# Local attention of the layers on packed columns: query blocks of 64 by 192 keys, cross blocks transposed in pairs, and values with exchanged halves

## The reference

```
def look_around(t):                     # the window before a window's own
    p = jnp.pad(t, ((0, 0), (0, 0), (1, 0), (0, 0), (0, 0)))
    return jnp.concatenate([p[:, :, :w], p[:, :, 1:]], axis=3)
sim = jnp.einsum('bhwid,bhwjd->bhwij', bq, bk)       # 128 queries, 256 keys
mask = (i < j) | (i > j + WINDOW) | (j == -1)
attn = jax.nn.softmax(jnp.where(mask, -jnp.finfo(sim.dtype).max, sim), axis=-1)
out = jnp.einsum('bhwij,bhwjd->bhwid', attn, bv)
...
h = shift_token(x); qkv = h @ wqkv; q, k = rotary_xpos(l2norm(q) * qs, l2norm(k) * ksc)
x = x + local_attention(q, k, v) @ wo
h = layernorm(shift_token(x)); a, g = jnp.split(h @ w1 + b1, 2, axis=-1)
x = x + (a * gelu(g)) @ w2 + b2
```

## Time and profile before

| | us |
|---|---|
| runs of the kernel | 2047.69 median of 3 (2045.26 to 2047.88) |
| the profiled execution | 2045.3, of it the span 2043.5 |
| busy: PE | 1900.0 (93%) |
| ACT | 1386.6 (68%) |
| DVE | 1327.4 (65%) |
| POOL | 960.7 (47%) |

### The profile page before, as it was taken

One profiled execution on the slowest core, in us unless ns is written; L12 is line 12 of the kernel. 1 busy time (PEld: TensorE's weight loads), 2 busy tenths in 40 slices (PEclk: granted clock), 3 DMA queues, 4 the chain that ended last, 5 costly groups with the idle time before them and its releaser, 6 DMA issues.

```text
span 2043.5 us, 42506 instructions
## 1 busy us (share of the span) xinstructions
PE 1900.0 (93%) x15184; PEld 1576.0 (77%) x15184; DVE 1327.4 (65%) x4125; ACT 1386.6 (68%) x3869; POOL 960.7 (47%) x1311
## 2 busy tenths in 40 slices
PE   6999999999999789999999999999999999999998
PEld 4778777777777668778788787787887878878777
DVE  4544543444443467777768777787777776877775
ACT  5886877778678465775766757657567575675764
POOL 2432442434243463644726537457265473663732
PEclk9999999999999889999999999999999999999999
DMA  3322231313225411010110101304101011010010
GB/s 127 109 80 66 75 118 44 97 60 88 92 66 162 151 39 32 19 43 12 45 45 12 42 22 37 104 6 161 55 6 52 22 45 55 22 42 27 31 33 27
DMA packets 122261, 121.10 MB, mean 59 GB/s; under 512 B 27188, under 2 KB 100804, under 8 KB 122052
## 3 DMA queue, kind: packets, MB, share of 16 engines
q1 hardware_dynamic: 118884, 112.10, 17.2%
q10 hardware_dynamic: 3168, 6.29, 0.9%
HBM read 72.72 MB, written 37.25 MB: 54 GB/s over the span
## 4 chain that ended last, share of the span: by engine, by line
PE 32%; DVE 20%; ACT 9%; issue 3%; POOL 3%; DVEq 0%; ACTq 0%; SPq 0%; POOLq 0%
PE f_bank L1383 11%; PE f_scores L1523 5%; PE f_scores L1461 4%; ACT f_prob L1598 4%; DVE f_u L1751 4%; PE f_bank L1509 4%; PE f_bank L1469 4%; DVE f_gu L1748 2%; PE f_o_bank L1484 2%; ACT f_u L1618 2%; PE f_bank L1434 2%; DVE y_tok L1734 2%; DVE y_tok L1740 1%; POOL f_prob L1336 1%; DVE f_rstd L1727 1%
## 5 line engine op out<-in xcount | busy, mean ns | idle before, releaser
L1336 POOL TENSOR_SCALAR f_prob<-f_prob,f_row_inv 128x256 f32<-128x256 f32 x512 | 263.0, 532 | 331.2 <-DVE f_row_inv L1694 331.1
L587 POOL TENSOR_SCALAR a_prob<-a_prob,a_row_inv,a_gate 128x128 f32<-128x128 f32 x512 | 224.4, 455 | 407.8 <-DVE a_row_inv L927 407.8
L1383 PE MATMUL f_bank<-weights,f_actT 128*128 128x512 f32 x1152 | 301.8, 406 | 1.6 <-DVE f_actT L1637 1.6
L1509 PE MATMUL f_bank<-f_hT,f_w 128*128 128x256 f32 x2112 | 276.2, 286 | 7.6 <-DVE f_gu L1748 7.6
L1509 PEld LDWEIGHTS f_bank<-f_hT,f_w 128*128 128x128 f32 x2112 | 261.9, 190 | 14.2 <-DVE f_gu L1748 10.7
L1598 ACT ACTIVATE f_prob<-f_scores,f_neg_max 128x256 f32<-128x256 f32 x512 | 235.8, 487 | 32.6 <-DVE f_neg_max L1686 31.6
L1383 PEld LDWEIGHTS f_bank<-weights,f_actT 128*128 128x128 f32 x1152 | 208.4, 191 | 50.3 <-ACT f_probT L1545 5.4
L1686 DVE CUSTOM_DVE_ANT_0 f_scores<-f_scores,f_mask 128x256 f32<-128x256 f32 x512 | 199.8, 456 | 14.8 <-PE f_scores L1461 14.7
L1312 POOL TENSOR_TENSOR f_norm<-f_norm,f_minus_half 128x16 f32<-128x16 f32 x64 | 198.6, 3104 | 21.5 <-DVE f_norm L1646 18.9
L1618 ACT ACTIVATE f_u<-f_gu 128x256 fp32r<-128x256 f32 x192 | 80.2, 418 | 179.4 <-DVE f_gu L1748 179.4
L819 ACT ACTIVATE a_prob<-a_scores,a_neg_max 128x128 f32<-128x128 f32 x512 | 179.5, 390 | 27.8 <-DVE a_neg_max L918 26.5
(11 more groups left out here) (129 smaller groups left out, 3834.5 us busy)
## 6 DMA issues: line engine op xcount, KB each, us to landing
split_weights<-a_hi_lo SPq DMA_DIRECT2D x16, 512.0 KB, 2.8
x_next<-states SPq DMA_DIRECT2D x32, 256.0 KB, 3.2
tables<-scaled_tables SPq DMA_DIRECT2D x16, 512.0 KB, 6.2
f_x<-states SPq DMA_DIRECT2D x16, 512.0 KB, 5.5
split_weights<-a_hi_lo SPq DMA_DIRECT2D x12, 682.0 KB, 4.2
weights<-split_weights ACTq DMA_DIRECT2D x6, 1024.0 KB, 9.7
f_w<-split_weights SPq DMA_DIRECT2D x4, 1280.0 KB, 10.8
a_x_tok<-in_x SPq DMA_DIRECT2D x8, 512.0 KB, 4.4
```

The costliest lines, as they stand in the source:

```text
L587: last = nc.gpsimd.tensor_scalar(part, part, row_inv[:, a % 2, head, t:t + 1], gate[:, half, t, h:h + 1], ALU.mult, ALU.mult)
L1336: last = nc.gpsimd.tensor_scalar(part, part, row_inv[:, a % 2, head, t:t + 1], 1.0, ALU.mult, ALU.mult)
L1383: last = nc.tensor.matmul(out, lhs(c, a), rhs(c, b), start=(i == 0), stop=(i == len(order) - 1))
L1509: mm = nc.tensor.matmul(out[:, which * PART:(which + 1) * PART], w1[:, wp, c, col:col + P], hT[:, hp, c, columns_of(a // FH)], start=(i == ...
```

## The change

The mapping of a unit's work changes, for the layers alone; the gated part is as before.

- **Scores.** Instead of 4 products (64 rows, 128 queries, 256 keys) there are 12 of 64 queries each: 192 keys for one block of 64 queries of a tile, 128 + 64 for the other. In the packed 192 columns, the 128 keys of the tile that a block of queries needs whole lie together, and so do the other 64 ("cross": the two blocks of queries of a tile take them from different tiles and different halves).
- **Mask, exponential, weigh** work on 192 columns. The mask becomes three tables of 192.
- **Transposes.** 3 per head and unit instead of 4: one of 128 columns for each tile's whole part, and one for the cross blocks of both tiles (64 + 64 columns).
- **Copies.** The transposed bank goes to `probT` in three ACT instructions per head: 128 partitions by 4x64 for the whole parts (named `own` in the code), then the cross blocks with 64 partitions by 2x64 each, for partitions 0 to 63 and 64 to 127, to different columns. `copied` is raised by the last.
- **Values.** 256 + 64 + 64 + 64 + 64 columns for a unit instead of 256 + 128 + 128 (the first unit of a pair in the first half of a sequence: 256 + 64 + 64). Two of the products take their values from `v_crossed`, which holds values with the two 64-token halves of tiles exchanged.
- **Exchange.** A new step `cross_values` of SP fills `v_crossed` for the next half by four transfers of 64x512 numbers (128 KB each) within SBUF, after `project_v` of that half, and in SP's order behind `shift_back` and ahead of `load_wqkv` and `out`. `v_crossed` is one buffer.
- **Square.** `square` has one slot instead of two: ACT's squares of k wait until DVE has summed those of q, and those of the next q until DVE has summed k's.
- **Start.** POOL clears `probT` and part of `v_crossed` once, at the layers' start.

The diff, cut to its core:

```diff
+BLOCK = P // 2
+KEYS = P + BLOCK
...
+         ("up", 3), ("rope", 3), ("x1_bias", 0), ("down", 1), ("down", 2), ("transpose_h", 1), ("cross_values", 0), ("load_wqkv", 0), ("up", 4),
+         ("up", 5), ("down", 3), ("add_attended", 0), ("up", 6), ("up", 7), ("up", 8), ("up", 9), ("rope_sum", 3), ("down", 4),
...
+        PACKED = (((FIRST, slice(0, KEYS), 0), (SECOND, slice(P, 2 * P), 0), (SECOND, SECOND, P)),
+                  ((SECOND, slice(BLOCK, 2 * P), 0), (FIRST, slice(0, P), BLOCK), (FIRST, slice(P, KEYS), 0)))
...
+        v_crossed = sb("v_crossed", [P, 2, F_INNER])
+        probT = sb("probT", [P, 2, 2, 8 * BLOCK])
         hT = sb("hT", [P, 2, CT, CHUNK], F32R)
         u = sb("u", [P, 2 * TILES, 2, PART], F32R)
...
-        square = sb("square", [P, 2, CHUNK])
+        square = sb("square", [P, CHUNK])
...
+            def cross_values(it, h):
+
+                half = prepared(it, h)[1]
+                sp.wait_ge(copied.sem, copied.past(it, ("project_v", (h + 1) * TILES - 1)))
+                sp.sem_inc(sp_carried, 1)
+                if half:
+                    sp.dma_start(v_crossed[FIRST, 0], values_of(half, -1)[SECOND]).then_inc(v_crossing.sem, 16)
+                else:
+                    sp.sem_inc(v_crossing.sem, 16)
+                sp.dma_start(v_crossed[SECOND, 0], values_of(half, 1)[FIRST]).then_inc(v_crossing.sem, 16)
+                sp.dma_start(v_crossed[FIRST, 1], values_of(half, 1)[SECOND]).then_inc(v_crossing.sem, 16)
+                sp.dma_start(v_crossed[SECOND, 1], values_of(half, TILES - 1)[FIRST]).then_inc(v_crossing.sem, 16)
...
             pool.memset(minus_half[:], -0.5)
+            pool.memset(v_crossed[FIRST, 0], 0.0)
+            pool.memset(probT[:], 0.0)
...
                         pe.wait_ge(exped.sem, exped.past(it, ("scores", a - 2), 1) if a >= 2 else exped.upto(it, -1))
                         for t in (0, 1):
                             col = (tile + t) * P
-                            for head in (0, 1):
-                                rows = slice(DH * head, DH * (head + 1))
-                                mm = nc.tensor.matmul(scores[a % 2][head][:, t, :], q[rows, pair, col:col + P],
-                                                      kT[rows, pair, col:col + 2 * P], start=True, stop=True)
+                            for queries, keys, place in PACKED[t]:
+                                for head in (0, 1):
+                                    rows = slice(DH * head, DH * (head + 1))
+                                    mm = nc.tensor.matmul(scores[a % 2][head][queries, t, place:place + keys.stop - keys.start],
+                                                          q[rows, pair, col:col + P][:, queries],
+                                                          kT[rows, pair, col:col + 2 * P][:, keys], start=True, stop=True)
                         mm.then_inc(scored.sem, 1)
...
-                            for j in range(4):
-                                last = nc.tensor.transpose(out[:, j * P:(j + 1) * P], prob[:, a % 2, head, j // 2, (j % 2) * P:(j % 2 + 1) * P],
-                                                           ident[:])
+                            packed = prob[:, a % 2, head].rearrange("p t k -> p (t k)")
+                            for place, source in enumerate((0, 2 * P, P)):
+                                last = nc.tensor.transpose(out[:, place * P:(place + 1) * P], packed[:, source:source + P], ident[:])
...
+                        if a % UNITS == 0:
+                            pe.wait_ge(v_crossing.sem, v_crossing.past(it, ("cross_values", half - 1)) if half else v_crossing.upto(it, -1))
...
-                        order = [(tile, P, 3 * P, 0, 2 * P), (tile + 1, 3 * P, 4 * P, P, 2 * P)]
+                        place = pair % 2 * PART
+                        crossed = v_crossed[:, tile // 2]
+                        order = [(values_of(half, tile), 2, 0, 2 * P), (values_of(half, tile + 1), 6, P + BLOCK, BLOCK), (crossed, 0, P, BLOCK)]
                         if half or tile:
-                            order = [(tile - 1, 0, P, 0, P)] + order
-                        turn, place = a % 2 * 4 * P, pair % 2 * PART
-                        for i, (key_tile, p0, p1, o0, o1) in enumerate(order):
+                            order += [(crossed, 7, BLOCK, BLOCK), (values_of(half, tile - 1), 1, 0, BLOCK)]
+                        for i, (operand, block, o0, n) in enumerate(order):
                             for head in (0, 1):
-                                mm = nc.tensor.matmul(o_bank[DH * head:DH * (head + 1), place + o0:place + o1],
-                                                      value_operand(half, key_tile, pair, head), probT[:, head, turn + p0:turn + p1],
+                                col = (2 * pair + head) * DH
+                                mm = nc.tensor.matmul(o_bank[DH * head:DH * (head + 1), place + o0:place + o0 + n], operand[:, col:col + DH],
+                                                      probT[:, head, a % 2, block * BLOCK:block * BLOCK + n],
                                                       start=(i == 0), stop=(i == len(order) - 1), skip_group_check=True)
                         mm.then_inc(o_filled.sem, 1)
...
-                    nc.scalar.activation(place, like(bank[n % 3], place), ACT.Copy).then_inc(copied.sem, 1)
+                    if kind == "transpose":
+                        own = bank[n % 3][:, 0:2 * P].rearrange("p (t b n) -> p t b n", t=2, b=2)
+                        cross = bank[n % 3][:, 2 * P:3 * P].rearrange("p (b n) -> p b n", b=2)
+                        nc.scalar.activation(place[:, 1:7].rearrange("p (t k) n -> p t k n", t=2)[:, :, 0:3:2], own, ACT.Copy)
+                        nc.scalar.activation(place[FIRST, 2:8:5], cross[FIRST], ACT.Copy)
+                        nc.scalar.activation(place[SECOND, 0:6:5], cross[SECOND], ACT.Copy).then_inc(copied.sem, 1)
+                    else:
+                        nc.scalar.activation(place, like(bank[n % 3], place), ACT.Copy).then_inc(copied.sem, 1)
...
-                    if ("project_qk", a - 1) in emptied.firsts(it):
-                        act.wait_ge(emptied.sem, emptied.past(it, ("project_qk", a - 1), which))
+                    if which == KEY:
+                        act.wait_ge(emptied.sem, emptied.past(it, ("project_qk", a), QUERY))
+                    elif ("project_qk", a - 1) in emptied.firsts(it):
+                        act.wait_ge(emptied.sem, emptied.past(it, ("project_qk", a - 1), KEY))
                     elif it is not None:
                         act.wait_ge(emptied.sem, emptied.upto(it, -1))
-                    nc.scalar.activation(square[:, which, :], bank[(first + which) % 3][:], ACT.Square).then_inc(raw_taken.sem, 1)
+                    nc.scalar.activation(square[:], bank[(first + which) % 3][:], ACT.Square).then_inc(raw_taken.sem, 1)
...
-                                last = nc.scalar.activation(prob[:, a % 2, head, t, :], scores[a % 2][head][:, t, :], ACT.Exp,
+                                last = nc.scalar.activation(prob[:, a % 2, head, t, :], scores[a % 2][head][:, t, 0:KEYS], ACT.Exp,
...
-                                sc = scores[a % 2][head][:, t, :]
-                                last = nc.vector.tensor_tensor_reduce(out=sc, in0=sc, in1=mask[:, min(half * TILES + tile + t, 1)], scale=-1.0,
+                                sc = scores[a % 2][head][:, t, 0:KEYS]
+                                last = nc.vector.tensor_tensor_reduce(out=sc, in0=sc, in1=mask[:, t + 1 if half or tile or t else 0], scale=-1.0,
```

37 lines of the change are left out of this document (19 added, 18 removed).

## The result

The changed kernel takes 2063.49 us in the median of 4 runs (2063.24 to 2064.2), the kernel before beside it 2046.47: a ratio of 1.009, 95% interval 1.0077 to 1.0102. The change makes the kernel 0.9% slower. Its profiled span is 2061.5 us, 18.0 more than before.

A forecast was written before the change was run, and what follows sets the result against it. TensorE, fed through ScalarE's copies, was taken to bound the attention stretches, both engines nearly full in the first. +0.85 us a half, 16 times, gave 13.6 on 2045.3, 2058.9, plus one for the median: 2060 us; range 2032 to 2084.

The forecast's parts named there:

- the walk: Delays followed through one half's queues: project_o +0.75 us, transpose_h +0.85, carried by the MLP; 16 x 0.85 = 13.6 us.
- ScalarE's copies and the square wait outweigh TensorE's gain: The forecast itself, in the attention stretches: slower, 2060 us, with bounds 2052 to 2078; chance 0.50.
- Copies: ScalarE's three copies a head: 0.85 us against 0.478, +0.37, because copies of 64 partitions do not overlap.
- Square: One slot makes k's squares wait for DVE's sum: 0.3 to 0.5 us in the first project_qk, +1.4 in the third.
- The rival in which DVE's shorter masks shrink the long wait to some tenths: Gain and loss cancel, as DVE sums earlier in the third project_qk: 2044 to 2052 us; chance 0.15.
- Scores: TensorE's scores of a unit: 0.99 us instead of 1.13, -0.14; -0.26 with full overlap, +0.38 without.
- The rival in which the blocks of queries do not overlap: TensorE's scores cost +0.38 us a unit instead of -0.14: 2090 us; chance 0.08.
- Transposes: TensorE's transposes: two of eight records a unit dropped, -0.22 us.
- values: TensorE's value products: same column count in more, shorter products, 0 to +0.10 us a unit, taken as +0.05.
- Exchange and clears: SP's four transfers hidden by 30 us of cover, POOL's clears by its waiting: nothing; clears at worst +5 us.
- The same walk without the square wait comes to about zero: Through the half, without the wait for DVE's sums, TensorE's gain and ScalarE's extra time were to cancel.
- The faster rival: ScalarE's short copies overlap, +0.15 us a head instead of +0.37: 2030 to 2043 us; chance 0.20.

The follow-up runs named there:

- e3: The changed kernel with the second head's copies of a unit reordered: partitions 64 to 127, then the whole part, then 0 to 63; 1.0003 of the kernel before.
- e2: The kernel before with one slot for the squares instead of two, nothing else changed; 1.0087 of the kernel before.
- e8: The changed kernel with the exchange of values run only once, before the first half, waits kept; 1.0098 of the kernel before.
- e1: The changed kernel with two slots for the squares again, the second in the MLP's idle gu buffer; 0.9958 of the kernel before.
- e6: The changed kernel with both two square slots and the second head's copies reordered (64 to 127, whole, 0 to 63); 0.9894 of the kernel before.

## Why the prediction was right

The time forecast was 2060, the time is 2063.5 (17.0 us more than the kernel before beside it, where the walk had 13.6), and the mechanism is the one forecast: ScalarE's copies and the square wait outweigh TensorE's gain. Point by point:

- *Copies.* 0.85 us a head, as summed. The reason that I gave, "A copy of 64 partitions doesn't" overlap, was wrong in its form: e3 shows that a changed start partition does it. In the earlier trace rows the two could not be told apart, since those copies start at different partitions in turn. The Trainium skill's page "ScalarE: Activation LUTs" (What ACT_TABLE_LOAD costs) lets activations back to back overlap by about 93 ns; the runs agree where the start stays (0.39 long, 0.28 apart) and not where it changes (0.27 long, 0.30 apart).
- *Square.* The wait of 1.24 us stands in the third `project_qk`, k's squares of which start 26.50 us into the half against 25.37 (medians over six halves of the kind that the walk goes through): +1.13, forecast +1.27. In the first `project_qk` the wait is 0.27, forecast 0.3 to 0.5. The rival in which DVE's shorter masks shrink the long wait to some tenths is out. That the slot's price is large shows in e2, +0.89 us a half in the kernel before.
- *Scores.* 0.89 instead of 1.13, -0.24: next to the bound of -0.26, where I took -0.14. The rival in which the blocks of queries do not overlap is out.
- *Transposes* gave the 0.22 forecast, and *values* stayed as they were (taken +0.05). Masks went from 456 to 390 ns as forecast; exponentials (487 to 424) and POOL (532 to 476) gave some 15 ns more than the middle that I had taken.
- *The walk.* `project_o` +0.84 (forecast +0.75), `transpose_h` +0.95 (+0.85), both in the half that was walked through, counted from its first record of scores. A whole half is longer by 1.04 at full clock and by 1.14 on average over seven, forecast +0.85. The walk took one half for all, but they are of two kinds: in the other, at full clock, k's squares come at 24.92 before and at 26.49 after, so they lose 1.57, and `project_o` (33.48 and 34.51) loses 1.03.
- *Exchange and clears.* The exchange costs nothing (e8; it lands in 2.3 us). No run leaves out the clears alone; in the trace of the changed kernel they take POOL 2.3 us while it waits, and POOL's next work for the layers comes 6.98 us after its last clear, so they cost nothing that the trace shows.

Two terms of the walk were mis-sized, in opposite senses. "The same walk without the square wait comes to about zero": e1 measured -0.42% there, -8.6 us. "+0.85 a half" for the whole thus hid what the wait costs: not 13.6 us, but 1.3% or 27. The gain that I missed lies in the first stretch. Without the waits, q's copy of the third `project_qk` starts 23.04 us into the half in e1 and 23.44 before, so 0.4 early, where the walk had it 0.35 late, 0.3 of that by the first square wait, and `project_o` at 32.78 against 33.67 (all this in the kind of half walked through; in the other q's copy starts at 23.00 before, level with e1). The scores near their bound and the 13 ns more that each exponential gives are part of it. How the rest divides, no run told apart. The mechanism was right, but that the time came out so near, with two errors in opposite senses, is in part luck.

The faster rival ("It decides as soon as a head's three copies take less than about 0.7 us") put its point well for the copies alone: at 0.72 a head, e3 is level with the kernel before. It takes the second slot beside them (e6) to be 1.1% faster than that kernel.

Left open is why the clock falls (below): it did so now and then in every run with the packed columns, and no run tells why.

## What to carry to other kernels

Work that is taken from the busiest engine counts only as far as the engine that feeds it keeps up: count for each removed product what its packing costs the copies behind it, and walk the queues of both. A buffer halved to make room is part of the change and can cost more than the change gains; look for the same room in a buffer that is idle at that time, or in what the packing itself saves. Keep ScalarE's instructions that start at the same partition next to each other; if a layout needs copies of half the partitions, ask first whether the product that reads them can take the halves instead.
